# The second mixer of a two-layer AdaLN block: gates folded into diagonal matrix products

## The chip, the cores and the metric

The kernel runs on one core of a Trainium2 chip. The metric is the device time of one execution in microseconds. A core has five engines that work side by side and meet only through semaphores: TensorE (matrix products), VectorE, ScalarE, GpSimd (called POOL in the profile) and SyncE (SP), which here only starts DMAs. ScalarE and POOL start DMAs as well. Each engine, and each DMA queue, works through its own instructions in program order.

## The reference, cut to what matters

x is [4, 512, 512]: four batches of 512 tokens with 512 features. Two layers follow each other, and each modulates a LayerNorm with per-batch rows that come from a small product (`mod`):

```
for layer in (0, 1):
    sa, ca, ga, sb, cb, gb = rows of silu(c) @ wmod          # per batch, 512 each
    ga, gb = sign(.) * max(abs(.), 0.25)
    h = layernorm(x) * (1 + ca) + sa
    x = x + ga * mixer(h)
    h = layernorm(x) * (1 + cb) + sb
    x = x + gb * ffn(h)
```

Layer 0 has linear attention as its mixer and a mixture of experts as its feed-forward part. Layer 1 has a 2:4-sparsified gated feed-forward part, and this mixer, which is the subject here:

```
y = h @ M            # M = W_in.T * coefficients @ W_out.T, 512 x 512, made on the chip
mixer(h) = h + y * rsqrt(mean(y*y) + eps) * norm_w
```

So the second mixer's step is x + ga\*h + ga\*norm_w\*normalised(y).

## The kernel before, in words

The program has stages: A (attention, eight head groups in a loop, four batches in each), a front part with the router, 39 expert slots, `back()`, then stage C (the second mixer, `step_c(b)` for four batches b) and stage D (the last feed-forward part: four groups g of its inner columns, four batches in each, `step_d(g, b)`). `walk` calls the same sequence of functions for each engine, and each engine's version of `step_c` or `step_d` holds that engine's instructions in the order in which they run; this written order and the semaphores are all that schedules the work. A batch is four tiles (NT) of 128 tokens; the features are four chunks (NC) of 128.

Every float32 product is made from three fp32r products: both operands are split into a high and a low part, and `mm3` (L720 to L722) issues high\*high, high\*low and low\*high. The high part is written by ScalarE, the low part by VectorE or POOL.

Two PSUM banks, `TAIL`, form a ring whose places are numbered ahead by `plan_ring`. `ring_full` counts what TensorE has put into it, `ring_read` what has been read out, `ring_done` what is finished. A LayerNorm takes four places (four chunks transposed), in two halves. The chain of one LayerNorm (k, b), where k is 2 for the mixer of layer 1 and 3 for its feed-forward part, is:

1. VectorE: `bn_stats` (L1453) and `bn_aggr` over the batch, then the reciprocal root by three Newton steps on a 128x4 tile (L1431 to L1437, 11 small operations with the one that adds epsilon), each waiting for the one before it.
2. VectorE: `ln_apply` (L1476), (x - mean) \* rstd into `xn` (a view of `xnb`) or, for (2, 2) and (2, 3), into `xw`.
3. TensorE: the transposes (L751) into the ring.
4. ScalarE: `ln_out`, scale and bias (L1137, out of PSUM into `tmp`), then the high part of `hT` (L1141). POOL: the low part (L1982).

In `back()` TensorE makes M (L1006, in two halves), ScalarE and VectorE split it, and (2, 0) and (2, 1) are normalised. `step_c(b)` on TensorE makes y for four tiles (48 products, operands `M_` and `hT`) in six banks (`YB`) and then the transposes of the next LayerNorm, (2, 2), (2, 3), (3, 0), (3, 1) in turn. ScalarE squares y with a running sum. VectorE does steps 1 and 2 of the LayerNorm, a second root chain for y, and the scale pass (L1902) into `yn`, which POOL adds to x (L2253). The term ga\*h is made apart from that by `gated(b)` on VectorE: it multiplies the normalised tile by one row (L1508) and adds another (L1511), four operations each, and POOL adds the result to x (L2035). The rows (`crow`) are broadcast from DRAM to 128 partitions by DMAs of ScalarE's queue, three per batch. They are made by POOL in the first head group of stage A (`mod_rows`).

`step_d(0, 0)` and `step_d(0, 1)` still carry LayerNorms (3, 2) and (3, 3). A step of D has four product groups r (24 products for gate and up, L720 to L722 with `W1a` or `W1b`), silu on ScalarE (L1379), the product on VectorE (L1917), absolute values on ScalarE (L1371), the 2:4 selection on VectorE (L1935 to L1962), the high part `ad` on ScalarE (L1398), the low part on POOL, and one step later the tail: the down product, which uses `ad`, row scale and add to x. The weights of group 0 are split by ScalarE and POOL (`split_d`): quarters 0 and 1 during `step_c(2)`, 2 and 3 during `step_c(3)`.

On SP's queue the last head group of stage A issues row loads (L597) and reloads of x (L561); `back()` waits for the last expert sums and brings x back from DRAM (L683).

## Time and profile before

| | us |
|---|---|
| median of three timed runs | 2017.32 (2016.87 to 2019.9) |
| profiled execution, its own time | 2017.79 |
| its span | 2016.0 |
| TensorE busy | 1815.1 (90%) |
| VectorE busy | 1232.9 (61%) |
| ScalarE busy | 688.4 (34%) |
| POOL busy | 734.3 (36%) |

The times inside the span, here and in the rows below, count from the span's start. Busy shares are averages over stages with different limits, so the stage in question has to be read by itself: M is made from 1284 to 1312 us, stage C runs from 1337 to 1421 us, and stage D follows to the end. In a timeline row the columns are start, duration, engine, line, operation, output<-inputs and count; square brackets hold the idle time of the engine before it and what ended that. Several equal instructions in a row are merged into one with their count.

### The profile page before, as it was taken

What the parts mean: (1) busy time and instruction counts of PE and PEld (TensorE: products, weight loads), DVE (VectorE), ACT (ScalarE), POOL (GpSimd) and SP (SyncE); (2) the same over time, 40 slices, a digit from 0 to 9 for tenths busy, and PEclk for the clock granted to TensorE, in tenths of its full rate; (3) what the DMA queues carried; (4) which work ended last, traced back from release to release, by engine and by line L of the source; (5) the groups of instructions that cost most, each with busy time, mean ns of one, the idle gap of its engine ahead of it and who ended that gap; (6) DMA issues with size and microseconds to landing.
All of it is one profiled execution on the core that took longest, in us unless ns stands there. A gap on an engine that the chain in (4) does not pass through costs nothing.

```text
span 2016.0 us, 25506 instructions
## 1 busy us (share of the span) xinstructions
PE 1815.1 (90%) x8300; PEld 1423.6 (71%) x8300; DVE 1232.9 (61%) x2172; ACT 688.4 (34%) x1321; POOL 734.3 (36%) x717
## 2 busy tenths in 40 slices
PE   8989999999999999987549898957689999999996
PEld 5657888888888888866447676535477778787784
DVE  4557666666666666687754344389775757566564
ACT  2434454544454444432202232134333122213220
POOL 1436121212111122211343555357645445536442
PEclk9999999999999999998759999978799999999998
DMA  6211454535353535421387999600101011101011
GB/s 235 84 64 60 137 158 136 156 109 154 93 168 103 188 105 188 115 69 37 105 276 202 295 266 253 167 26 20 55 26 33 26 32 48 31 6 52 6 53 42
DMA packets 100194, 220.54 MB, mean 109 GB/s; under 512 B 6684, under 2 KB 31276, under 8 KB 98576
## 3 DMA queue, kind: packets, MB, share of 16 engines
q1 hardware_dynamic: 76160, 167.64, 26.3%
q0 software_dynamic: 11616, 28.98, 6.2%
q10 hardware_dynamic: 12336, 22.89, 3.7%
q8 instruction: 44, 0.72, 0.2%
q14 instruction: 38, 0.31, 0.0%
HBM read 128.11 MB, written 91.37 MB: 109 GB/s over the span
## 4 chain that ended last, share of the span: by engine, by line
PE 69%; DVE 18%; issue 6%; DMA 3%; ACT 2%; POOL 2%; ACTq 0%; POOLq 0%; DVEq 0%; SPq 0%
PE bank L720 21%; PE bank L722 20%; PE bank L721 20%; DVE hh L1962 2%; PE bank L911 2%; PE bank L786 2%; PE bank L1006 1%; DVE st L1453 1%; DVE rr L1723 1%; DMA u_d<-yt,sm 1%; PE bank L937 1%; DVE fl L1940 1%; DVE tmp L1715 1%; DVE na L1435 1%; DVE na L1434 1%
## 5 line engine op out<-in xcount | busy, mean ns | idle before, releaser
L1723 DVE RECIPROCAL rr<-rr 128x256 f32<-128x256 f32 x128 | 218.7, 1730 | 4.7 <-ACT num L1189 4.7
L720 PE MATMUL bank<-hT,W1b 128*128 128x512 f32 x512 | 210.5, 411 | 10.8 <-DVE hh L1917 10.8
L720 PE MATMUL bank<-W1a,hT 128*128 128x512 f32 x512 | 209.6, 409 | 3.4 <-DVE hT L1637 3.4
L721 PE MATMUL bank<-hT,W1b 128*128 128x512 f32 x512 | 205.1, 401 | 0.0
L722 PE MATMUL bank<-hT,W1b 128*128 128x512 f32 x512 | 204.8, 400 | 0.0
L722 PE MATMUL bank<-W1a,hT 128*128 128x512 f32 x512 | 201.4, 393 | 0.0
L721 PE MATMUL bank<-W1a,hT 128*128 128x512 f32 x512 | 200.7, 392 | 0.0
L2054 POOL TENSOR_TENSOR x<-x,tmp 128x512 f32<-128x512 f32 x64 | 101.3, 1583 | 261.3 <-DVE tmp L1715 261.3
L1917 DVE TENSOR_TENSOR hh<-hh,bank 128x512 f32<-128x512 f32 x64 | 43.2, 686 | 188.6 <-PE bank L722 159.2
L1742 DVE SCALAR_TENSOR_TENSOR kt<-bank,kt 128x256 fp32r<-128x256 f32 x128 | 50.8, 397 | 173.5 <-ACT vt L1205 173.4
L1982 POOL TENSOR_TENSOR W<-stage,W 128x1024 fp32r<-128x1024 f32 x32 | 76.8, 2400 | 189.6 <-ACT W L1097 187.3
L1204 ACT ACTIVATE kt<-bank 128x256 fp32r<-128x256 f32 x128 | 49.3, 385 | 235.1 <-PE bank L722 234.5
L1398 ACT ACTIVATE ad<-hh 128x512 fp32r<-128x512 f32 x64 | 40.3, 633 | 253.1 <-DVE hh L1962 253.1
L720 PE MATMUL bank<-W1b,ot 128*128 128x512 f32 x256 | 105.3, 412 | 22.8 <-DVE tmp L1712 14.2
L720 PEld LDWEIGHTS bank<-hT,W1b 128*128 128x128 f32 x512 | 98.3, 192 | 35.2 <-DVE hh L1917 13.7
L720 PEld LDWEIGHTS bank<-W1a,hT 128*128 128x128 f32 x512 | 96.9, 189 | 36.9 <-issue 16.3
L722 PEld LDWEIGHTS bank<-hT,W1b 128*128 128x128 f32 x512 | 98.0, 191 | 24.2
L721 PEld LDWEIGHTS bank<-hT,W1b 128*128 128x128 f32 x512 | 98.3, 192 | 20.0
L722 PEld LDWEIGHTS bank<-W1a,hT 128*128 128x128 f32 x512 | 96.8, 189 | 22.1
L720 PE MATMUL bank<-W,ad 128*128 128x512 f32 x256 | 102.8, 402 | 10.1 <-DVE ad L1969 8.9
L721 PEld LDWEIGHTS bank<-W1a,hT 128*128 128x128 f32 x512 | 97.4, 190 | 17.6
L1776 DVE SCALAR_TENSOR_TENSOR qt<-bank,qt 128x512 fp32r<-128x512 f32 x64 | 44.0, 690 | 101.5 <-ACT qt L1233 101.5
(265 smaller groups left out, 4596.8 us busy)
## 6 DMA issues: line engine op xcount, KB each, us to landing
hs_d<-bor SPq DMA_DIRECT2D x24, 1548.0 KB, 11.9
ws_d<-W SPq DMA_DIRECT2D x48, 512.0 KB, 6.2
WB<-ws_d SPq DMA_DIRECT2D x8, 3072.0 KB, 17.5
stage<-wa SPq DMA_DIRECT2D x32, 512.0 KB, 5.5
stage<-wbe SPq DMA_DIRECT2D x24, 512.0 KB, 4.3
stage<-wdn SPq DMA_DIRECT2D x24, 512.0 KB, 3.9
mw<-wmod SPq DMA_DIRECT2D x10, 1024.0 KB, 4.8
hg<-hs_d ACTq DMA_DIRECT2D x39, 258.0 KB, 4.5
```

The lines of the kernel that those rows point to most:

```text
L720: pe.matmul(o, lhs(HI), rhs(HI), start=start, stop=False, **kw)
L721: pe.matmul(o, lhs(HI), rhs(LO), start=False, stop=False, **kw)
L722: return pe.matmul(o, lhs(LO), rhs(HI), start=False, stop=stop, **kw)
L786: last = pe.matmul(o[0:NB, :], scT[:, layer, c, :], w[:, c * H:(c + 1) * H], start=c == 0, stop=c == NC - 1)
L911: last = pe.matmul(bank[NN[pair][head]][:, :], kvb[q, wl, pair, :], qt[q, wr, pair, :], start=i == 0, stop=i == 2)
L1204: act.activation(kt[:, t % 2, HI, :], bank[t % 2][:, 0:256], ACT.Relu)
L1723: dve.reciprocal(rr[:, pair, h], rr[:, pair, h]).then_inc(r_rec, 1)
L1742: dve.scalar_tensor_tensor(out=kt[:, t % 2, LO, :], in0=bank[t % 2][:, 0:256], scalar=0.0, in1=kt[:, t % 2, HI, :].bitcast(F32), op0=ALU.m ...
L1776: dve.scalar_tensor_tensor(out=qt[:, LO, pair, :], in0=bank[pair][:, :], scalar=0.0, in1=qt[:, HI, pair, :].bitcast(F32), op0=ALU.max, op1 ...
L1917: dve.tensor_tensor(hh[:, r, :], hh[:, r, :], bank[4 + r % 2][:, :], ALU.mult).then_inc(d_h, 1)
L1982: return pool.tensor_tensor(dst, src, hi.bitcast(F32), ALU.subtract)
L2054: pool.tensor_tensor(xt, xt, tmp[:, (key + t) % 2, :], ALU.add).then_inc(ring_done, 1)
```

## The change

- **The term ga\*h** is no longer made by VectorE and POOL. TensorE multiplies h (the same `hT` columns that feed y) by a diagonal matrix of ga per batch and chunk (`gated_h`): for each of four tiles, four chunks of 128 columns with three products each, into four ring places called "res". VectorE adds each place to x. The 16 diagonals (`dg`) are written by ScalarE (identity times a gate column) and VectorE (low part) in `back()`. The gate columns (`gcol`) come by four element-wise DMAs of SP's queue in the last head group. `gated`, `gated_add` and two of three broadcast rows go; the third is now loaded by SP (`crow_load`).
- **The LayerNorms (2, \*) and (3, \*)** are applied by ScalarE: Identity with scale rstd and bias -mean\*rstd, from x (`ln_scaled`).
- **Shared chains**: `c_scales` computes the reciprocal roots of one or two LayerNorms and of y in one chain on a wider tile, and the bias with one operation more. In `step_c` that chain stands behind the squares of y.
- **The normalised y** is added to x by VectorE and not by POOL.
- **Order**: the transposes of (3, 1), (3, 2), (3, 3) go into `step_d(0, 0)`, behind groups 0, 1 and 3, and `step_c(3)` has none. `step_d(0, 1)` carries no LayerNorm any more, so its absolute values follow each group. Weight quarters 0 and 1 are split at the start of `back()`, 2 and 3 behind the last "res" product of `step_c(3)`, because `dg` lies where `W1b` will be. `YB` has another order of banks, so that group 0 of D waits for 12 reads of y and group 1 for 16.

The diff, cut to its core. TensorE:

```diff
+            def gated_h(b):
+                n0 = RING[("res", b)]
+                pe.wait_ge(dg_lo, NC * (b + 1))
+                for t in range(NT):
+                    o = ring_slot(n0 + t, (n0 + t) % 2)
+                    for c in range(NC):
+                        last = mm3(o[:, c * P:(c + 1) * P], hcol(c, b, t), lambda h, c=c: dg[:, b, h, c, :],
+                                   c == 0, c == NC - 1, skip_group_check=True)
+                    last.then_inc(ring_full, 1)
...
                     last.then_inc(y_full, 1)
+                gated_h(b)
                 for half in range(2):
-                    ln_transposes(layernorms("C", 0, b), half)
+                    ln_transposes(C_LNS[b], half)
```

ScalarE:

```diff
             def back():
-                for i in range(SLOTS - NY, SLOTS):
-                    act.wait_ge(us_done[i % NY], added(i))
-                crows(0, 0)
-                crows(1, 0)
+                act.wait_ge(dn_full, SLOTS)
+                split_d(0, 0)
+                split_d(0, 1)
+                act.wait_ge(gcol_full, 16 * NB)
+                for b in range(NB):
+                    for c in range(NC):
+                        act.activation(dg[:, b, HI, c, :], ident[:, :], ACT.Copy, scale=gcol[:, c, b:b + 1]) \
+                            .then_inc(dg_hi, 1)
...
+            def ln_scaled(k, b):
+                p = (k - 2) * NB + b
+                act.wait_ge(c_scaled, p + 1)
+                if p >= 2:
+                    act.wait_ge(ring_full, ln_end(2 + (p - 2) // NB, (p - 2) % NB))
+                col = column((k, b))
+                for t in range(NT):
+                    last = act.activation(xn_of(k, b)[:, t, :], x[:, b * NT + t, :], ACT.Identity,
+                                          scale=crs[:, col + t:col + t + 1], bias=cnm[:, col + t:col + t + 1])
+                last.then_inc(xn_ready, 1)
...
+            def step_c(b):
+                if b > 0:
+                    ln_scaled(*((2, 3), (3, 0), (3, 1))[b - 1])
+                squares(b)
+                if b == 0:
+                    ln_scaled(2, 2)
+                if b == 3:
+                    act.wait_ge(ring_full, RING[("res", 3)] + NT)
+                    split_d(0, 2)
+                    split_d(0, 3)
+                if C_LNS[b]:
+                    ln_out(C_LNS[b], 0)
+                    ln_out(C_LNS[b], 1)
```

VectorE:

```diff
             def step_c(b):
-                ln = layernorms("C", 0, b)
-                stats(ln, range(NT))
-                ln_apply(*ln)
...
+                if b == 0:
+                    c_stats(2, 2)
+                    c_stats(2, 3)
+                    c_scales((2, 2), (2, 3), ("y", 0))
+                else:
+                    c_stats(3, b - 1)
+                    c_scales((3, b - 1), ("y", b))
+                n0 = RING[("res", b)]
+                for t in range(NT):
+                    n = n0 + t
...
+                    dve.wait_ge(ring_full, n + 1)
+                    xt = x[:, NT * b + t, :]
+                    dve.tensor_tensor(xt, TAIL[n % 2][:, :], xt, ALU.add).then_inc(ring_read, 1)
...
-                if gated_in("C", 0, b) is not None:
-                    gated(gated_in("C", 0, b))
+                for t in range(NT):
+                    n = NT * b + t
+                    dve.wait_ge(y_read, n + 1)
+                    xt = x[:, n, :]
+                    dve.tensor_tensor(xt, xt, yn[:, t, :], ALU.add).then_inc(c_add, 1)
```

POOL:

```diff
             def step_c(b):
-                for t in range(NT):
-                    n = NT * b + t
-                    pool.wait_ge(y_read, n + 1)
-                    xt = x[:, NT * b + t, :]
-                    pool.tensor_tensor(xt, xt, yn[n % 4], ALU.add).then_inc(c_add, 1)
-                ln_out(ln, 0)
-                ln_out(ln, 1)
...
-                gated_add(gated_in("C", 0, b))
+                n0 = RING[("res", b)]
+                for t in range(NT):
+                    pool.wait_ge(ring_done, n0 + t)
+                    pool.wait_ge(ring_read, n0 + t + 1)
+                    pool.tensor_tensor(mark[:, 2:3], mark[:, 0:1], mark[:, 1:2], ALU.add).then_inc(ring_done, 1)
```

## Rows read from the trace of the kernel before

**Rows 1.** Windows of two stretches: span, busy us (instructions) by engine, granted clock, DMA share, GB/s.

```profile
1312.00:1337.20 25.20, 5.98 (x32) 4.47 (x31) 18.05 (x33) 9.09 (x15) 13.09 (x10) 0.61 0.08 21
1337.20:1421.60 84.40, 58.73 (x258) 46.19 (x256) 80.69 (x169) 34.34 (x66) 56.14 (x39) 0.85 0.13 38
```

**Rows 2.** Waits of TensorE, 1284 to 1500 us: total, times, longest.

```profile
PE bank L751 <- DVE xnb L1476: 47.0, 4, 17.3
```

**Rows 3.** Groups on VectorE, 1284 to 1500 us: busy, mean ns, idle before.

```profile
L1511 DVE TENSOR_TENSOR xw<-xw,crow 128x512 f32<-128x512 f32 x8 | 14.8, 1904 | 0.0
L1508 DVE TENSOR_TENSOR xw<-xw,crow 128x512 f32<-128x512 f32 x8 | 12.7, 1648 | 0.0
...
L1508 DVE TENSOR_TENSOR xnb<-xnb,crow 128x512 f32<-128x512 f32 x8 | 11.1, 1448 | 6.5 <-PE bank L751 6.5
L1511 DVE TENSOR_TENSOR xnb<-xnb,crow 128x512 f32<-128x512 f32 x8 | 9.3, 1220 | 0.0
```

**Rows 4.** Timeline of TensorE's products.

```profile
1311.79 1.04 PE L751 MATMUL bank<-ident,xnb 128*128 128x128 f32 x8
...
1333.09 3.15 PE L751 MATMUL bank<-ident,xnb 128*128 128x128 f32 x12 [17.30 <-DVE xnb L1476]
...
1337.22 0.78 PE L720 MATMUL bank<-M_,hT 128*128 128x512 f32 x1
...
1374.68 0.40 PE L722 MATMUL bank<-M_,hT 128*128 128x512 f32 x1
1374.91 0.40 PE L720 MATMUL bank<-M_,hT 128*128 128x512 f32 x1
...
1421.65 0.47 PE L720 MATMUL bank<-hT,W1a 128*128 128x512 f32 x1 [0.84 <-issue]
...
1475.38 0.79 PE L720 MATMUL bank<-hT,W1b 128*128 128x512 f32 x1 [2.97 <-DVE hh L1917]
1475.97 0.63 PE L721 MATMUL bank<-hT,W1b 128*128 128x512 f32 x1
1476.39 0.63 PE L722 MATMUL bank<-hT,W1b 128*128 128x512 f32 x1
...
1494.01 0.47 PE L720 MATMUL bank<-W,ad 128*128 128x512 f32 x1 [1.01 <-ACT tmp L1137]
```

**Rows 5.** Timeline of 130-column products in stage A, and a weight load (PEld) among them.

```profile
600.12 0.28 PE L722 MATMUL bank<-vt,kt 128*128 128x130 f32 x1
600.24 0.27 PE L720 MATMUL bank<-vt,kt 128*128 128x130 f32 x1
...
600.17 0.19 PEld L720 LDWEIGHTS bank<-vt,kt 128*128 128x128 f32 x1
```

**Rows 6.** Groups on ScalarE, whole span, forms apart.

```profile
L1204 ACT ACTIVATE kt<-bank 128x256 fp32r<-128x256 f32 x128 | 49.3, 385 | 235.1 <-PE bank L722 234.5
...
L1137 ACT ACTIVATE tmp<-bank,modc 128x512 f32<-128x512 f32 x48 | 37.0, 771 | 83.6 <-issue 33.1 <-PE bank L751 25.2 <-POOL hT L1982 24.9
```

**Rows 7.** Costliest groups of the page: VectorE out of PSUM.

```profile
L1917 DVE TENSOR_TENSOR hh<-hh,bank 128x512 f32<-128x512 f32 x64 | 43.2, 686 | 188.6 <-PE bank L722 159.2
```

**Rows 8.** Timeline of VectorE.

```profile
1298.33 1.88 DVE L1453 BATCH_NORM_STATS2 st<-x 128x6 f32<-128x512 f32 x3 [13.05 <-DMA x<-u_d]
...
1405.54 1.21 DVE L1434 TENSOR_TENSOR na<-ve,rstd 128x4 f32<-128x4 f32 x1
1406.78 0.16 DVE L1435 SCALAR_TENSOR_TENSOR na<-na,rstd 128x4 f32<-128x4 f32 x1
...
1462.14 0.68 DVE L1935 TENSOR_TENSOR fl<-xnb 128x512 bf16<-128x512 f32 x1
```

**Rows 9.** Timeline of SP's DMA issues.

```profile
880.78 0.38 SPq L561 DMA_DIRECT2D x<-x_in  x1
```

**Rows 10.** Timeline of ScalarE, the last write of batch 1's LayerNorm.

```profile
1339.34 0.63 ACT L1141 ACTIVATE hT<-tmp 128x512 fp32r<-128x512 f32 x1
```

**Rows 11.** Timeline of POOL during the held operation of VectorE.

```profile
1404.19 2.54 POOL L1982 TENSOR_TENSOR hT<-tmp,hT 128x512 fp32r<-128x512 f32 x2
```

More of the change, by code:

```diff
@@ L125, in mod_uses, with column @@
     return ([(i - 1, "col")] if i > 0 and MOD_PARTS[i - 1] in COL_KIND else []) + [(i, "row")]
-def gated_in(stage, g, b):
-    return {1: 2, 3: 3}.get(b) if stage == "C" else None
+def column(what):
+    return NT * STATS.index(what)
 def tail_of(stage, g, b):
@@ L165, in plan_ring @@
                     halves = [("ln", *ln, 0), ("ln", *ln, 1)]
-                    parts = {"A": halves[:1] + parts + halves[1:], "C": parts + halves, "D": halves + parts}[stage]
+                    parts = halves[:1] + parts + halves[1:]
+                if stage == "C":
+                    parts = [("res", b)] + ([("ln", *C_LNS[b], h) for h in range(2)] if C_LNS[b] else [])
+                if (stage, g, b) == ("D", 0, 0):
+                    parts = [("ln", *ln, h) for ln in D_LNS.values() for h in range(2)]
                 if stage == "A" and g == 0:
@@ L1046, in step_d @@
                     need_h(3, b)
[L1047 to L1048 removed]
                 for r in range(4):
+                    if first and b == 0 and r < 2:
+                        pe.wait_ge(y_read, (NT * NB - 4, NT * NB)[r])
                     if b == 0:
@@ L1366, in absolute @@
                     if r == 0:
-                        if ln:
-                            act.wait_ge(ring_full, ln_end(*ln))
-                        if not (first and b == 0):
+                        if first and b == 0:
+                            act.wait_ge(ring_full, ln_end(3, 3))
+                        else:
                             act.wait_ge(d_sp, s * NSP)
@@ new lines, in matrix_lo @@
+            def matrix_lo(half):
+                for j in range(2):
+                    m = 2 * half + j
+                    dve.wait_ge(m_hi, m + 1)
+                    dve.tensor_tensor(M[:, LO, m, :], bank[((0, 1), (4, 5))[half][j]][:, :], M[:, HI, m, :].bitcast(F32),
+                                      ALU.subtract).then_inc(m_lo, 1)
+            def back():
+                diagonals()
+                c_stats(2, 0)
+                c_scales((2, 0))
+                matrix_lo(0)
+                c_stats(2, 1)
+                c_scales((2, 1))
+                matrix_lo(1)
@@ L2265, in step_d @@
                         split_d(g + 1, j)
-                ln = layernorms("D", g, b)
-                ln_out(ln, 0)
-                ln_out(ln, 1)
+                if isinstance(g, int) and g == 0 and b == 0:
+                    for ln in D_LNS.values():
+                        ln_out(ln, 0)
+                        ln_out(ln, 1)
                 tails("D", g, b)
```

251 lines of the change are left out of this document (116 added, 135 removed).

## The prediction

> **What bounds the kernel now.** The slices of the page show TensorE busy nearly everywhere except in two dips, and the later one is the second mixer and the start of the last stage, so I cut that stretch into windows. From 1337.2 to 1421.6 us VectorE is busy 80.7 of 84.4 us while TensorE is busy 58.7, and TensorE's granted clock is 0.61 in the stretch ahead and 0.85 in this one [rows 1]. The waits of TensorE say the same: 47.0 us of them were ended by VectorE's LayerNorm apply into one buffer alone, in four stops of up to 17.3 us [rows 2]. VectorE's groups in the same stretch show what stands in front of that apply: two passes over a gated tile per batch, 14.8 + 12.7 + 11.1 + 9.3 = 47.9 us in 32 operations [rows 3]. So here a microsecond off VectorE's queue is a microsecond off the end, until TensorE's own order takes over. After 1494 us TensorE runs without a stop worth the name, and whatever moves 1494.01 earlier moves the end by as much [rows 4].
>
> The sum is made against the profiled execution, 2017.8 us, of which 2016.0 are span. That is 0.5 us above the median of the three timed runs, 2017.3. 0.2%, what a measurement can tell from no change, is 4 us.
>
> **The change, part by part.**
>
> *Removed from VectorE:* the eight gated operations per batch, 48 us in all, the four-operation apply, and one of two reciprocal-root chains per batch (11 operations, 0.2 us apart when nothing holds them). *Removed from POOL:* the gated add and the add of the normalised output, 32 operations of the size of its subtractions, 1.27 us each at best.
>
> *Added to TensorE:* 48 small products per batch (4 tiles, 4 chunks, 3 precision parts, 128 columns). The nearest rows are products of 130 columns with the same weight load, which start 0.11 us apart (600.12 and 600.24) [rows 5]: 48 x 0.112 = 5.4 us a batch, 21.6 in all. The bounds are 0.06 us each (a quarter of the 0.23 us of 512 columns [rows 4]; 2.9 us a batch) and 0.19 us each, the weight load's own record (9.1 us a batch). I take 0.112, since width and operands are nearly equal. The Trainium skill, "TensorE: Matmul & The Clock Gate", section "The mechanism", says that a weight load overlaps products in flight only when its row group differs. Rival D works that case out from rows.
>
> *Added to ScalarE:* 32 applies of 128x512 with scale and bias. The nearest row is the same function at 0.77 us [rows 6], so 3.1 us a batch; bounds 0.6 and 0.8. Sixteen diagonals of 128x128: below the 0.385 us of 128x256 [rows 6], about 0.27, 4.3 us. VectorE's 16 low parts: well below the 0.69 us of 128x512 [rows 7], about 0.3, 5 us. These and the two weight splits moved in front of them (2 us on ScalarE, 4.9 on POOL) lie between the last expert product at 1284 and the landing of x, which starts VectorE at 1298.33 after 13.05 idle us [rows 8]. I take their cost as nothing; if the cover went, they would still be under TensorE's matrix product, which runs to 1311.8.
>
> *Added to VectorE:* per batch four adds out of PSUM and four scale passes (0.69 each [rows 7]) and four adds with both inputs in SBUF, 0.68 each alone (the first step of the selection, 1462.14) [rows 8].
>
> *DMA and queues:* four loads of the gate columns, 2048 single elements, on SP's queue in the last head group. They stand ahead of the reload of x that is issued at 880.78 [rows 9] and waits for the tail of an earlier batch, by some 25 us (a head group's step): nothing, and each of the four would have to take 6 us to reach it. Twelve row broadcasts leave ScalarE's queue, four come on SP's; each has 18 us before its use. POOL's row arithmetic in the first head group shrinks by three operations off the path.
>
> **Leg 1, matrix product to first output product.** Before: 1311.79 to 1337.22. The transposes of batch 0 stay where they are. ScalarE needs 6.9 us from their start to its last write (1333.09 to 1339.34 + 0.63 in the next batch [rows 4, 10]), so it is free at 1318.7, applies batch 1's LayerNorm in 3.1, and the transposes then take 4.1 (1333.09 to 1337.22). First product at 1326.0: 11.2 us earlier. The matrix product itself and the wait for x are untouched.
>
> **Leg 2, the four steps.** TensorE's queue is in order: output products (48 x 0.23 = 11.0 us), gated tiles, transposes. Gated tiles 0 and 1 need 2.7 us, but tile 2 needs tile 0's bank back, and VectorE reads it only behind its shared chain: square 1.0 after the last product, chain 12 x 0.2 = 2.4, add 0.7, handover 0.1, so tile 2 starts at +4.2 instead of +2.7. Tiles 2 and 3 end at +6.9, VectorE's last read at +7.7, ScalarE's alternation with the transposes frees TensorE at +10.5. A step is 21.5, and I add 1 for stretches at the lower of the two clock levels (1.2 and 2.4 GHz), which show as products 0.43 us apart (1475.97 to 1476.39, after a stop of 2.97 us) instead of 0.23 [rows 4]: 22.5. Three steps and a last one without transposes (11 + 7): 85.5, so the last stage begins at 1411.5. Before, this leg took 84.4 (1337.22 to 1421.65 [rows 4]). The products that the change adds use up what the idle time gives back: this leg is worth -1 us. VectorE's own turn is 7.7 + 2.7 + 5.7 (adds beside POOL) + 2.9 (statistics) = 19 us, inside 22.5 with 3 to spare.
>
> **Leg 3, to the first tail.** Before: 72.4 us (1421.65 to 1494.01), with a stop for batch 2's LayerNorm in it. Now four product groups (5.5 each, 24 x 0.23) and three transposes (4.1), twice 1.0 waiting for ScalarE's apply: 36.3, to 1447.8. Late next is the 2:4 selection: ScalarE ends the LayerNorm writes at 1450.6, has two absolute values at 1451.9, and from there to the released product of the next batch it took 13.2 us before (1462.14 to 1475.38 [rows 4, 8]): 1465.1. TensorE has done the next two groups at 1458.8 and stands 6.3 us, where it stood 2.97. The next two groups then take 14.1 instead of 11, as they did at 0.43 us apart. First tail at 1479.2, before 1494.0.
>
> Sum: 11.2 - 1.1 + 4.7 = 14.8 us. **Forecast 2017.8 - 14.8 = 2003.0.**
>
> **The rivals.**
>
> *A, VectorE still bounds the steps (chance 0.20).* The turn of 19 us holds only if the SBUF adds cost 1.4 us. The gated passes beside POOL averaged 1.2 to 1.9 [rows 3]. At 1.9, and with some of the statistics' small operations held, the turn is 24 to 25, the step about 25: 3 x 2.5 later, 2010.5. Against it: POOL has lost half of its work.
>
> *B, the chain is held on TensorE's path (0.06); this one ends slower.* A two-input operation took 1.21 us where the next one took 0.16 [rows 8], while POOL's subtractions of 1.27 us were running [rows 11]. The chain now stands between the output products and gated tile 2 in every step. The Trainium skill, "SBUF — State Buffer", Terms, says the port pair of VectorE and GpSimd is locked for a whole instruction and the loser blocks; by that rule the trace agrees. If 8 of 12 operations are held in each step, 8 x 1.05 x 4 = 34 us: 2037. It decides from 14.8 / 4 = 3.7 us a step, four held operations. Against: POOL's subtractions for a batch end about 8 us before the next chain starts.
>
> *C, the last stage gives it back (0.07).* If the selection is held by POOL as well, the stop of 6.3 us becomes 12: 2009.
>
> *D, weight loads don't overlap (0.02).* Each small product would cost 0.19 + 0.11 = 0.30 us, 14.4 a batch instead of 5.4, 36 us over four: 2024. The rows exclude it as far as 130-column products go: a load of 0.19 us lies inside products that start 0.11 apart [rows 5]. By the skill's sentence it would be so; the trace does not agree.
>
> *E, smoother than I count (0.15).* No step at the lower clock and the stop in leg 3 under 3 us: 3 + 3 + 3 less, 1994 to 1998. The change not doing what it says can be excluded: the passes are gone from VectorE's queue.
>
> **How the numbers follow.** Forecast case 0.50 (1998 to 2008), A 0.20, E 0.15, C 0.07, B 0.06, D 0.02. Range 1996 to 2012: it takes the forecast case, C, most of A and E. Faster by over 0.2% (below 2013.3): 0.50 + 0.15 + 0.07 + 0.16 of A = 0.88. Same: 0.05, from A's upper end and a mild B. Slower: 0.07.
>
> **What would show it.** Right: the first output product near 1326, steps of 21.5 to 23.5 us, small products 0.11 us apart, the last stage from about 1411, the first tail near 1479, TensorE's waits for the LayerNorm apply almost gone. Wrong: small products over 0.15 us apart; chain operations of over 1 us between the squares and the first PSUM add; steps of 25 with VectorE full; a diagonal ending after 1311; the first tail later than 1488.

## The result, and the profile after

The changed kernel takes 2002.79 us (median of four runs, 2002.44 to 2004.78), the kernel before 2017.09 us on the same chip. The ratio is 0.9924, with a 95% interval of 0.9909 to 0.9939, so the kernel is faster by 0.76%. The span of the profiled run fell from 2016.0 to 2000.9 us, by 15.1. All medians and ratios, here and below, are of executions in the faster of the two states that a core shows; one execution of the kernel with one product part (2108.9 us) and one of the kernel before (2327.1) were in the slower one and are left out.

To compare kernels I cut their traces at the same four products of TensorE. The **segment** runs from the first product of the matrix M to the first tail product of the last stage. It has three legs, as in the prediction: up to the first output product, the four steps of stage C, and the last stage up to its first tail. Below is the timeline of TensorE after the change, with the marks of these legs and the rows between them that the argument needs.

```profile
1283.36 0.59 PE L1030 MATMUL bank<-mst 128*128 128x512 f32 x1
...
1320.56 3.15 PE L775 MATMUL bank<-ident,xnb 128*128 128x128 f32 x12 [5.74 <-ACT xnb L1373]
...
1324.33 0.48 PE L744 MATMUL bank<-M_,hT 128*128 128x512 f32 x1
...
1335.41 0.22 PE L744 MATMUL bank<-dg,hT 128*128 128x128 f32 x1
...
1335.58 0.28 PE L746 MATMUL bank<-dg,hT 128*128 128x128 f32 x1
1335.69 0.27 PE L744 MATMUL bank<-dg,hT 128*128 128x128 f32 x1
...
1339.58 0.33 PE L744 MATMUL bank<-dg,hT 128*128 128x128 f32 x1 [1.38 <-DVE x L1970]
...
1340.75 0.41 PE L745 MATMUL bank<-dg,hT 128*128 128x128 f32 x1
1340.96 0.42 PE L746 MATMUL bank<-dg,hT 128*128 128x128 f32 x1
...
1347.70 0.48 PE L744 MATMUL bank<-M_,hT 128*128 128x512 f32 x1
...
1411.97 0.73 PE L744 MATMUL bank<-hT,W1a 128*128 128x512 f32 x1
...
1466.76 0.79 PE L744 MATMUL bank<-hT,W1b 128*128 128x512 f32 x1 [7.49 <-DVE hh L1989]
...
1479.72 0.39 PE L744 MATMUL bank<-W,ad 128*128 128x512 f32 x1
```

The kernel before started M at 1284.33. With [rows 4] the legs are:

| | before | after | forecast |
|---|---|---|---|
| leg 1, M to first output product | 52.9 | 41.0 (-11.9) | -11.2 |
| leg 2, the four steps | 84.4 | 87.6 (+3.2) | +1.1 |
| its steps | 21.5, 15.4, 25.9, 21.6 | 23.4, 22.8, 22.2, 19.3 | 22.5 three times, 18 |
| leg 3, to the first tail | 72.4 | 67.8 (-4.6) | -4.7 |
| segment | 209.7 | 196.4 (-13.3) | -14.8 |

The rest of the 15.1 us is 1.0 ahead of M and 0.8 behind the first tail. The three legs of the changed kernel as windows (columns as in [rows 1]):

```profile
1283.36:1324.33 40.97, 33.31 (x98) 16.44 (x96) 28.05 (x78) 22.41 (x42) 13.40 (x12) 0.92 0.48 147
1324.33:1411.97 87.64, 81.89 (x436) 70.28 (x434) 52.95 (x114) 41.53 (x77) 25.95 (x31) 0.89 0.03 10
1411.97:1479.72 67.75, 55.07 (x241) 43.39 (x242) 31.87 (x53) 36.47 (x55) 31.11 (x21) 0.92 0.13 39
```

Against the second window of [rows 1], which is leg 2 of the kernel before, the idle engine is now VectorE: it is busy 53 of 87.6 us instead of 81 of 84.4, and TensorE 82 instead of 59. The waits of TensorE from 1270 to 1500 us (total, times, longest) answer to [rows 2]:

```profile
PE bank L744 <- DVE hh L1989: 7.5, 1, 7.5
PE bank L775 <- ACT xnb L1373: 6.4, 2, 5.7
PE bank L775 <- ACT tmp L1171: 6.0, 12, 1.0
PE bank L744 <- DVE x L1970: 5.1, 4, 1.4
```

The 47.0 us of waits for the LayerNorm apply into xnb have become 6.4. In their place stand four short stops, one a step, behind y's chain and the first residual add (`x L1970`), and one stop of 7.5 us in the last stage. VectorE and ScalarE in step 0, and VectorE's adds of the normalised output in step 1, from their timelines:

```profile
1336.40 0.17 DVE L1928 TENSOR_SCALAR cst<-csum 128x4 f32<-128x4 f32 x1 [17.35 <-ACT sqj L1383]
...
1338.73 0.17 DVE L1936 SCALAR_TENSOR_TENSOR cst<-cmv,cst 128x8 f32<-128x8 f32 x1
1338.84 1.29 DVE L1970 TENSOR_TENSOR x<-bank,x 128x512 f32<-128x512 f32 x2
...
1369.85 6.16 DVE L1982 TENSOR_TENSOR x<-x,yn 128x512 f32<-128x512 f32 x4
```

```profile
1317.59 2.91 ACT L1373 ACTIVATE xnb<-x,cst 128x512 f32<-128x512 f32 x4
```

The chain takes 2.4 us and no operation of it is held; an apply on ScalarE takes 0.73 us. VectorE's adds of the normalised output are another matter. While POOL makes the low parts of the next LayerNorm, four of them take 6.16 us, 1.54 each. In the run below in which VectorE applies LayerNorm, the same four in step 0 take 2.49 us.

### The profile page after: what moved, and what is told of

Its sections match the earlier page's. It is cut to its first block and busy times, and to the rows that moved or that the text cites. A ratio compares the mean times of both kernels' runs of the same rounds, so it can differ in the third digit from the quotient of the medians.

```text
span 2000.9 us, 25863 instructions
## 1 busy us (share of the span) xinstructions
PE 1842.2 (92%) x8492; PEld 1450.2 (72%) x8492; DVE 1191.6 (60%) x2112; ACT 716.7 (36%) x1369; POOL 686.3 (34%) x697
## 5 line engine op out<-in xcount | busy, mean ns | idle before, releaser
L744 PE MATMUL bank<-hT,W1b 128*128 128x512 f32 x512 | 208.9, 408 | 14.8 <-DVE hh L1989 14.8
L744 PE MATMUL bank<-W1a,hT 128*128 128x512 f32 x512 | 209.7, 410 | 3.4 <-DVE hT L1657 3.4
L1989 DVE TENSOR_TENSOR hh<-hh,bank 128x512 f32<-128x512 f32 x64 | 43.4, 686 | 195.4 <-PE bank L746 166.0
L744 PE MATMUL bank<-W1b,ot 128*128 128x512 f32 x256 | 104.8, 410 | 23.0 <-DVE tmp L1732 14.8
```

The lines of the kernel that those rows point to most:

```text
L744: pe.matmul(o, lhs(HI), rhs(HI), start=start, stop=False, **kw)
L1989: dve.tensor_tensor(hh[:, r, :], hh[:, r, :], bank[4 + r % 2][:, :], ALU.mult).then_inc(d_h, 1)
```

## The experiments

Each run is compared with the kernel before on its own chip. On these chips it took 2018.7 us (the two edits of the kernel before, the adds on POOL, LayerNorm on VectorE), 2019.0 (both moves taken back), 2021.4 (chains separate, residual adds first, the two earlier LayerNorms) or 2021.0 (the other three), so the medians can't be compared with each other, only the ratios. The segment is that of one profiled execution. Leg 1 repeats well (41.0 in the runs that leave it alone, 41.3 in three of them). Leg 3 is 66.4 to 68.0 us in the changed kernel and the four runs that edit neither it nor the adds and applies ahead of it, so a difference of about 1 us in a segment says little. The whole times need several executions each, since what lies outside the segment scatters by more.

| run | median us | ratio, 95% interval | leg 1 | leg 2 | leg 3 | segment |
|---|---|---|---|---|---|---|
| before | 2017.1 | 1 | 52.9 | 84.4 | 72.4 | 209.7 |
| before, gated term left out | 1987.9 | 0.985 (0.983 to 0.987) | 42.8 | 71.6 | 60.1 | 174.5 |
| before, adds on VectorE | 2012.3 | 0.996 (0.995 to 0.998) | 52.8 | 81.1 | 67.5 | 201.4 |
| **changed** | 2002.8 | 0.992 (0.991 to 0.994) | 41.0 | 87.6 | 67.8 | 196.4 |
| adds on POOL | 2007.4 | 0.994 (0.991 to 0.997) | 41.0 | 92.3 | 69.5 | 202.7 |
| LayerNorm on VectorE | 2002.7 | 0.992 (0.990 to 0.993) | 37.4 | 93.0 | 64.0 | 194.3 |
| both moves taken back | 2005.7 | 0.993 (0.992 to 0.994) | 37.4 | 94.0 | 65.2 | 196.6 |
| chains separate | 2002.5 | 0.990 (0.989 to 0.992) | 41.0 | 86.4 | 68.0 | 195.4 |
| one product part of three | 1995.3 | 0.987 (0.985 to 0.989) | 41.3 | 81.6 | 67.1 | 190.0 |
| POOL kept busy | 2016.2 | 0.998 (0.997 to 0.999) | 41.3 | 101.1 | 68.0 | 210.4 |
| residual adds first | 1993.0 | 0.985 (0.984 to 0.987) | 41.3 | 76.2 | 69.1 | 186.7 |
| LayerNorm (2,1) earlier | 2001.8 | 0.991 (0.989 to 0.993) | 37.6 | 89.5 | 66.4 | 193.6 |
| LayerNorm (3,3) earlier | 1999.0 | 0.990 (0.988 to 0.993) | 41.0 | 87.8 | 64.1 | 192.9 |
| four changes of order | 1982.0 | 0.981 (0.980 to 0.983) | 37.6 | 77.3 | 60.0 | 174.9 |

**What the gated term costs, in the kernel before.** The two passes, the gated add and their row loads are taken out:

```
 def gated(b):
     ...
-    for t in range(NT):
-        dve.tensor_tensor(xg[:, t, :], xg[:, t, :], crow[:, 0, :], ALU.mult).then_inc(pq_mul, 1)
-    for t in range(NT):
-        dve.tensor_tensor(xg[:, t, :], xg[:, t, :], crow[:, 1, :], ALU.add).then_inc(pq_sum, 1)
 def gated_add(b):
     ...
-        pool.tensor_tensor(xt, xt, xn_of(2, b)[:, t, :], ALU.add).then_inc(pq_add, 1)
```

> The kernel before, with the term ga*h left out: the gated passes of VectorE, their adds on POOL and their row loads are gone, everything else stays (so x misses that term). Theory (the gated passes bound the old stage): the first output product comes about 12 us earlier, a step of stage C falls from 21 to about 16 us, the stop for the LayerNorm in the last stage shrinks; in all about 40 us less, 1977 us (1970 to 1985). Rival (the serial LayerNorm and root chains bound it, and the change won by moving and sharing them): less than 10 us gained, over 2007.

The segment is 35.2 us shorter, the kernel 30. That is less than the 40 expected, and 1988 us lies outside the range given, but far from the rival's 2007: the passes were on the path, as [rows 2, 3] had been read. 35.2 us for passes of 47.9 us says that part of them had cover; how much can't be had by subtraction, since the adds on POOL went too, and since durations hold waits (see the next run). With everything else left in its order, the 35.2 us bound what another way to compute ga\*h could win.

**One move alone, on the kernel before.** The normalised output is added by VectorE, behind its scale pass:

```
 def step_c(b):                       # VectorE
     ...
+    ...                              # for b < 3 behind POOL's gated add of the same batch
+    for t in range(NT):
+        dve.tensor_tensor(xt, xt, yn[n % 4], ALU.add).then_inc(c_add, 1)
 def step_c(b):                       # POOL
-        pool.tensor_tensor(xt, xt, yn[n % 4], ALU.add).then_inc(c_add, 1)
```

> The kernel before, with one part of the change alone: the normalised y is added to x by VectorE and not by POOL. Theory (VectorE bounds the old stage, so each operation put on it is paid): four adds more per batch at 0.7 to 1.4 us, 4 x 2.7 to 4 x 5.6 = 11 to 22 us, less what POOL's smaller load gives back: 2027 us (2022 to 2034). Rival (POOL's add is what delays the statistics of the next LayerNorm, so this part helps by itself): 2012 or less.

The theory of a slower kernel was wrong: it is faster, by 0.36%, and by 8.2 us in the segment. Sixteen more operations were put on the engine that bounds it, and it finished sooner. The groups on VectorE from 1284 to 1500 us (busy us, mean ns | idle before) show how:

```profile
L1911 DVE TENSOR_TENSOR x<-x,cs 128x512 f32<-128x512 f32 x8 | 14.0, 1785 | 0.0
...
L1911 DVE TENSOR_TENSOR x<-x,ct 128x512 f32<-128x512 f32 x8 | 10.7, 1381 | 0.0
...
L1508 DVE TENSOR_TENSOR xw<-xw,crow 128x512 f32<-128x512 f32 x8 | 7.2, 954 | 0.0
L1511 DVE TENSOR_TENSOR xw<-xw,crow 128x512 f32<-128x512 f32 x8 | 7.1, 946 | 0.0
L1434 DVE TENSOR_TENSOR na<-ve,rstd 128x4 f32<-128x4 f32 x36 | 5.8, 162 | 1.2
```

The adds cost 24.7 us. But the passes over xw fell from 27.5 us [rows 3] to 14.3, and the small operation of the chain from this row of the kernel before, same view, to half of it:

```profile
L1434 DVE TENSOR_TENSOR na<-ve,rstd 128x4 f32<-128x4 f32 x36 | 11.2, 310 | 1.2
```

With the other small operations the chains fell from 37.6 us to 22.6 (L1431 to L1437), and with the passes that is 28.2 us less, more than the adds cost. The rival, that POOL's add delays the next statistics, is not what the trace shows: VectorE has no wait for POOL in that stretch in either run, the time is in the durations. POOL had done its adds of 1.29 to 1.52 us during the passes and the chains; that these adds held both is the reading that fits, and the run with POOL kept busy tests it. The durations in a trace hold these waits, so the busy time of an engine isn't a quantity of work that can be added and subtracted.

**The same move, taken back from the changed kernel.**

```
-    for t in range(NT):              # VectorE
-        dve.wait_ge(y_read, n + 1)
-        dve.tensor_tensor(xt, xt, yn[:, t, :], ALU.add).then_inc(c_add, 1)
+    for t in range(NT):              # POOL, step_c, ahead of the LayerNorm's low parts
+        pool.wait_ge(y_read, n + 1)
+        pool.tensor_tensor(xt, xt, yn[:, t, :], ALU.add).then_inc(c_add, 1)
```

> The changed kernel, with that part alone undone: the normalised y is added to x by POOL, in front of its LayerNorm low parts, as it was before. Theory: POOL's adds end 15 to 16 us after the last output product instead of its low parts at 14, the low part of the first transposed chunk comes about 7 us later, and ScalarE may not fill the second place of its buffer before that; TensorE's transposes and with them three steps grow by about 6 us: 2020 us (2012 to 2026). Rival (VectorE's adds cost on its own turn, so giving them back helps): 2000 or less.

The direction held in the segment and the size did not: 6.4 us, not 17. The whole times alone can't tell this run from the changed kernel (0.991 to 0.997 against 0.991 to 0.994). POOL and ScalarE in step 0 and behind it, from their timelines, show the way it takes:

```profile
1343.29 5.01 POOL L2308 TENSOR_TENSOR x<-x,yn 128x512 f32<-128x512 f32 x4 [0.41 <-DVE yn L1975]
1348.26 2.54 POOL L2048 TENSOR_TENSOR hT<-tmp,hT 128x512 fp32r<-128x512 f32 x2
```

```profile
1349.67 0.78 ACT L1171 ACTIVATE tmp<-bank,modc 128x512 f32<-128x512 f32 x1 [4.12 <-POOL hT L2048]
...
1352.35 2.92 ACT L1373 ACTIVATE xnb<-x,cst 128x512 f32<-128x512 f32 x4
1355.17 0.57 ACT L1383 ACTIVATE sqj<-bank 128x512 bf16<-128x512 f32 x1
```

POOL's adds delay its low parts, these hold ScalarE's third eviction for 4.12 us, behind it stands the apply and behind the apply stand the four squares. So y's chain starts 1.6 us behind the first small product of step 1 instead of 1.0, the stop of TensorE for it is 1.88 us instead of 1.24, and tiles 2 and 3 take 4.4 us instead of 3.8.

**LayerNorm applied by VectorE**, the other move taken back:

```
-        last = act.activation(xn_of(k, b)[:, t, :], x[:, b * NT + t, :], ACT.Identity, scale=..., bias=...)
+        last = dve.tensor_scalar(xn_of(k, b)[:, t, :], x[:, b * NT + t, :], crs[...], cnm[...], ALU.mult, ALU.add)
```

> The changed kernel, with the LayerNorm apply of stages C and D back on VectorE (0.54 us an operation instead of 0.77 on ScalarE), shared chains and diagonal products kept. Theory (moving the apply was not what won, and in leg 1 it even costs, since ScalarE comes to batch 1's apply only behind batch 0's writes): first output product 4 us earlier, the first step 2 us longer since the apply stands behind the adds out of PSUM, 1 to 2 us less in the last stage: 2000 us (1996 to 2004). Rival (the apply on ScalarE is a main part of the gain): over 2008.

The whole time is as expected, its parts less so. The applies stand in VectorE's queue right behind their chains, but (2,2) behind the adds out of PSUM. Leg 1 is without the 3.6 us in which ScalarE applied (2,1) behind its evictions, and step 0 gives them back with interest: 28.4 us against 23.4, 5 us longer and not 2. Leg 3 is 3.7 us shorter and not 1 to 2. For the whole the move to ScalarE is worth nothing here: 194.3 against 196.4 us, and a ratio with nearly the same interval.

**Both moves taken back**, so that the diagonal products, the shared chains and the change's new order are left:

> The changed kernel with both of its moves taken back, LayerNorm applied by VectorE and the normalised output added by POOL, so that of the change the diagonal products (and the shared chains) alone are left. Theory (the parts add up, each read from the run in which it alone was taken back: 202.7 us with the add on POOL, 194.3 us with LayerNorm on VectorE, against 196.4 us): 202.7 - 2.0 = 200.7 us for the segment, 9 us less than the kernel before, and 2007 us (2004 to 2010). Rival (VectorE's applies and POOL's adds hold each other, as the kernel before showed with its adds on POOL; the two moves are worth more together than apart): a segment of 204 us or more, 2010 to 2016 us, with applies of LayerNorm of over 1 us each where POOL adds.

For the segment neither held: it is 196.6 us, the 196.4 of the changed kernel, where adding up had given 200.7. (The median of 2005.7 us lies in the theory's range, but the changed kernel would take some 2003.6 on this chip, and the two ratios overlap.) So **the two moves bring nothing together, and the rest of the change brings 13.1 of the 13.3 us**. The hold that the rival named did happen while POOL made its adds: four applies took 1.31 us each, where four others beside an idle POOL took 0.48. But with LayerNorm on VectorE and the adds left there, the same four took 1.48 beside POOL's low parts, so the adds on POOL brought no more of it. From VectorE's timeline of this run in step 0:

```profile
1354.58 5.25 DVE L1926 TENSOR_SCALAR xnb<-x,cst 128x512 f32<-128x512 f32 x4
```

What the two moves share may be ScalarE's slack. With the adds on POOL, ScalarE's evictions are still held for 3.6 us in this run, but no apply of 2.9 us stands behind them, and the chain of step 1 starts 1.0 us behind the first small product, as in the changed kernel. No run takes that slack alone, so this is a reading and not a test. The adds on VectorE are worth 6.4 us where ScalarE applies LayerNorm, and 2.3 (196.6 - 194.3) where it does not: the second move mostly pays for the first.

The 13.1 us look like a simple difference: the gated term costs 35.2 us in its old form, and in its new one 192 small products at 0.116 us, 22.3, which leaves 12.9. The legs show that this agreement is partly luck. Against the kernel before without the gated term, this run is 27.6 us longer in legs 2 and 3, not 22.3, and 5.4 us *shorter* in leg 1 (37.4 against 42.8), though neither has a pass there. Those 5.4 us come from a part of the change that its description does not name. In `back()` VectorE used to make the low parts of both halves of M before it turned to LayerNorm (2,1). Now (2,1) stands between the two halves, in time in which VectorE would wait for the second, and the transposes of (2,1) find their input ready. In the kernel before without the gated term TensorE still waits for it:

```profile
1325.25 1.11 PE L751 MATMUL bank<-ident,xnb 128*128 128x128 f32 x4 [7.23 <-DVE xnb L1464]
```

So of the 13.1 us an estimated 5.4 belong to this order and some 8 to the diagonal products with the rest (13.1 - 5.4 = 7.7). No run has the diagonal products in the old order, so the split is not tested.

**Chains separate:**

```
-                    c_scales((3, b - 1), ("y", b))
+                    c_scales((3, b - 1))
+                c_scales(("y", b))
```

> The changed kernel with separate root chains: the LayerNorm's before the wait for the squares of y, y's alone behind it. Theory (sharing saves VectorE operations that lie in its idle time, 3 to 4 us a step, so it is worth nothing here): from the start of the matrix product to the first tail product 196.4 us as in the changed kernel, within 1 us. Rival (sharing is a part of the gain, 2.2 us a step): 203 us or more.

The segment is 1.0 us shorter, at the edge of the 1 us that the theory allowed and as near to nothing as this can be read. The eleven operations that the shared chain saves lay in VectorE's idle time, which is 3 to 4 us a step.

**The price of the small products.** The gated product with one part of three (the two mixed ones left out):

```
-                        last = mm3(o[:, c * P:(c + 1) * P], hcol(c, b, t), lambda h, c=c: dg[:, b, h, c, :], ...)
+                        last = pe.matmul(o[:, c * P:(c + 1) * P], hcol(c, b, t)(HI), dg[:, b, HI, c, :], ...)
```

> The changed kernel with the gated output product ga * h computed from the high parts alone: 16 small products a batch instead of 48, so the two mixed terms of the split product are left out and the result is less exact. Theory (the small products cost 0.11 to 0.12 us each wherever TensorE has work, and lie on its path): 32 x 0.116 = 3.7 us less work a step; a part of it goes into the stop for y's chain, which VectorE sets, so 2 to 3.7 us a step and 8 to 13 us in all: 1990 to 1995 us. Rival (a step ends with VectorE's turn, and the small products only fill its wait): less than 3 us in all, 2000 to 2003.

The two measures differ. The segment is 6.3 us shorter, between theory and rival; the ratio is 0.987 against 0.992, about 11 us, inside the theory's 8 to 13, and the median of 1995.3 us is just past the range given. The profiled execution is the slowest of the three (2002.2, the others 1993.9 and 1995.3), and what the others won outside it is not known. In it, the waits of TensorE in the steps (1335 to 1420 us) say where most of the other 8.5 of the 14.8 us that 128 small products take went:

```profile
PE bank L1044 <- DVE x L1970: 12.3, 4, 3.2
```

The stop behind y's chain grew from 5.1 to 12.3 us. With fewer products TensorE mostly arrives earlier at a point that VectorE sets. That point, more than the number of small products, bounds the steps: the first three fell by 0.6 to 1.3 us each, and only the last, which has no transposes behind it, by 3.0.

**POOL kept busy beside the chain**, the price of rival B:

```
+                pool.wait_ge(y_sq, NT * (b + 1))
+                for _ in range(6):
+                    chained(pool.tensor_tensor(junk[:, :], junk[:, :], junk[:, :], ALU.add))
```

> The changed kernel with six additions of 128x256 bf16 on POOL, on a scratch tile that nothing reads, issued in each of the four steps as soon as the squares of the step are summed, beside y's chain on VectorE. Nothing waits for them. Theory (a VectorE instruction whose operands all lie in SBUF is held while one of POOL's runs): single operations of the chain take 0.4 to 1 us instead of 0.16, the chain 2 to 5 us longer, and TensorE's stop for x or for the gated tiles longer by as much: 1 to 4 us a step, 2007 to 2019 us. Rival (the operation of 2.37 us seen beside POOL's split in the run with the adds first has another cause): all operations of the chain stay at 0.16 us, 2002 to 2004 us.

The theory held: 2016.2 us, and 14.0 us more in the segment, 210.4 where the kernel before had 209.7. VectorE's and POOL's timelines in step 0:

```profile
1339.09 0.61 DVE L1929 TENSOR_SCALAR cst<-csum 128x4 f32<-128x4 f32 x1 [17.85 <-ACT sqj L1384]
1339.74 0.17 DVE L1931 TENSOR_SCALAR cst<-cst 128x12 int32<-128x12 int32 x1
1339.94 0.47 DVE L1933 TENSOR_TENSOR cst<-cst 128x12 f32<-128x12 f32 x1
1340.44 0.17 DVE L1934 SCALAR_TENSOR_TENSOR cst<-cst 128x12 f32<-128x12 f32 x1
1340.65 0.47 DVE L1935 SCALAR_TENSOR_TENSOR cst<-cst 128x12 f32<-128x12 f32 x1
1341.15 0.17 DVE L1933 TENSOR_TENSOR cst<-cst 128x12 f32<-128x12 f32 x1
```

```profile
1339.07 4.16 POOL L2309 TENSOR_TENSOR junk<-junk 128x256 bf16<-128x256 bf16 x6 [8.06 <-ACT sqj L1384]
```

Every second operation of the chain is held, and the one at its head too. Two of them with their gaps take 0.71 us (1339.94 to 1340.65), and POOL's additions come 0.69 us apart (six in 4.16): the chain runs at POOL's pace. 24 additions that nothing waits for, 16.6 us of POOL's time at that pace, and the gain in the segment is gone; of the whole time 0.2% of 0.8% is left. The Trainium skill, "SBUF — State Buffer", section "SBUF: two separate sides", says that a VectorE operation with two SBUF inputs and one of GpSimd lock the shared port pair for a whole instruction, and that whichever starts first blocks the other. The trace agrees for those operations. The held one at the head (`cst<-csum`, 0.61 us) has one input and is not of that kind; whether an addition of POOL was held in turn can't be read from it.

**The stop in each step taken out.** y's chain stands behind the four residual adds, which are what frees the banks for the gated tiles. For that it is separate from the LayerNorm's chain, as in the run with chains separate:

```
-                    c_scales((3, b - 1), ("y", b))
+                    c_scales((3, b - 1))
                 ...
                 for t in range(NT):
                     ...
                     dve.tensor_tensor(xt, TAIL[n % 2][:, :], xt, ALU.add).then_inc(ring_read, 1)
+                c_scales(("y", b))
```

> The changed kernel with separate chains, and VectorE's four adds out of the ring moved in front of y's chain. Theory (gated tile 2 waits for the add of tile 0 only because the chain stands before it, and the stop of 1.3 us also brings a stretch at the lower clock): the four stops of 1.25 to 1.38 us go, gated tiles 2 and 3 take 2.8 us each pair instead of 3.1 to 4.4, the stretch from the matrix product to the first tail product is 5 to 10 us shorter than 196.4. Rival (the two-bank ring or the transposes bound the step anyway): 195 or more.

Confirmed: 9.7 us less than the changed kernel and 8.7 less than the run with chains separate, with steps of 20.1, 19.9, 19.9 and 16.4, and the 48 small products of a batch in 5.5 us without a stop. In the run with chains separate the stops were these:

```profile
PE bank L744 <- DVE x L1971: 4.2, 4, 1.1
```

Leg 2 with the residual adds first, as a window:

```profile
1326.88:1403.09 76.21, 72.77 (x435) 62.72 (x433) 51.62 (x132) 40.99 (x76) 23.50 (x30) 1.00 0.03 11
```

For the same products TensorE is busy 72.8 us instead of 81.9, as its granted clock is 1.00 instead of 0.89 (with chains separate it is 0.89 too). In its last step POOL's weight splits met the chain. VectorE's and POOL's timelines:

```profile
1404.30 0.16 DVE L1932 TENSOR_TENSOR cst<-cst 128x4 f32<-128x4 f32 x1
1404.49 2.37 DVE L1933 SCALAR_TENSOR_TENSOR cst<-cst 128x4 f32<-128x4 f32 x1
1406.90 0.16 DVE L1934 SCALAR_TENSOR_TENSOR cst<-cst 128x4 f32<-128x4 f32 x1
1407.10 2.30 DVE L1932 TENSOR_TENSOR cst<-cst 128x4 f32<-128x4 f32 x1
```

```profile
1404.43 4.95 POOL L2054 TENSOR_TENSOR W1b<-stage,W1b 128x1024 fp32r<-128x1024 f32 x2
```

Two operations of the chain are held for 4.4 us, and TensorE stands 1.1 us for the normalised output ahead of the last stage's second group. So in the last step of the run with four changes two adds stand ahead of the chain and two behind it.

**ScalarE applies (2,1) right behind (2,0)**, where it waits for M's second half anyway:

```
                     if half == 0:
                         ln_scaled(2, 0)
+                        ln_scaled(2, 1)
                 ln_out((2, 0), 0)
                 ln_out((2, 0), 1)
-                ln_scaled(2, 1)
```

> The changed kernel with one line moved: ScalarE applies LayerNorm (2, 1) right behind (2, 0), while TensorE still makes the second half of M, and not behind the writes of (2, 0). Theory (the 2.9 us of that apply are on the path of leg 1): first output product 3.6 us earlier counted from the start of the matrix product, 37.4 us instead of 41.0, and the stretch to the first tail product 192.8. Rival (batch 0's low parts on POOL would hold the first output product anyway): 40 us or more.

Leg 1 is 37.6 us, as expected; of the 3.3 won, leg 2 takes 1.9 back. The segment of 193.6 us holds 1.4 in leg 3, which the edit doesn't touch.

**LayerNorm (3,3) one group earlier** in the last stage:

```
-D_LNS = {0: (3, 1), 1: (3, 2), 3: (3, 3)}
+D_LNS = {0: (3, 1), 1: (3, 2), 2: (3, 3)}
```

with its statistics behind the first product group instead of the second.

> The changed kernel with the last LayerNorm (3, 3) one product group earlier: its statistics behind VectorE's first product, its transposes behind group 2 instead of group 3. Theory (the absolute values, and with them the 2:4 selection, wait for its writes, and that makes the stop of 7.5 us before group 2 of the next batch): the stop falls to 3 or 4 us, the stretch to the first tail product is 3 to 5 us shorter than 196.4. Rival (the selection is late because of the last product group and not of the LayerNorm): the stop stays over 6 us.

Confirmed. The segment is 3.5 us shorter; the whole time (0.988 to 0.993) can't tell it from the changed kernel. The waits of TensorE from 1440 to 1500 us show the stop of 7.5 us as one of 4.1:

```profile
PE bank L744 <- DVE hh L1989: 4.1, 1, 4.1
```

**Four changes of order together:** the last three and this one, behind the squares of step 3:

```
                 squares(b)
+                if b == 3:
+                    ln_scaled(3, 2)
```

> The changed kernel with four changes of order together: the four residual adds stand ahead of y's chain in VectorE's queue (in the last step two ahead of it and two behind), ScalarE applies LayerNorm (2,1) right behind (2,0), it applies (3,2) right behind the squares of step 3, and (3,3) is emitted one group earlier in the last stage. Theory (each takes out a stop of its own, and the stops lie one behind another on TensorE): first output product 37.5 us behind the start of M's product instead of 41.0; steps of about 20, 20, 20 and 16 us instead of 23.4, 22.8, 22.3 and 19.3; 62 to 64 us from the last stage to the first tail instead of 67.8. The segment of 196.4 us falls to 176 to 180, the kernel to 1985 (1981 to 1989). Rival (the stops share a cause, so that one gain eats the other, for instance since ScalarE's applies now meet the gated evictions): no better than the adds ahead of the chain alone, a segment of 186.7 and 1993 us.

The theory held, a little on the good side: 1982.0 us, a segment of 174.9 (176 to 180 expected), which is 21.5 us less than the changed kernel and 34.8 less than before. Its legs 2 and 3 as windows:

```profile
1320.21:1397.46 77.25, 73.79 (x434) 63.44 (x433) 56.57 (x148) 43.83 (x80) 23.30 (x29) 0.98 0.04 11
1397.46:1457.48 60.02, 52.87 (x242) 42.07 (x242) 28.79 (x56) 33.72 (x51) 32.19 (x22) 0.97 0.15 45
```

In leg 2 TensorE is busy 73.8 us instead of 81.9 for the same products: its granted clock is 0.98 instead of 0.89. The single gains are 9.7, 2.8 and 3.5 us, 16.0 together. The other 5.5 are left for the apply of (3,2) and the split adds of the last step, which were not run alone, and for what the edits do to each other. What is left of waits from 1270 to 1480 us is mostly ScalarE's eviction of the transposes:

```profile
PE bank L775 <- ACT tmp L1171: 10.2, 18, 1.0
PE bank L744 <- DVE hh L1997: 3.0, 1, 3.0
```

## Why the prediction was right, and where its reasons were not

**The number** came out within 0.3 us of the median, 2003.0 against 2002.79. That is closer than its terms were, and the last microseconds of the agreement are luck. The legs erred by -0.7, +2.1 and +0.1 us, the changes outside the segment, -1.8 us, had been left out, and the two nearly cancel.

**What bounds the kernel.** That VectorE's passes stood on TensorE's path held. The sentence "a microsecond off VectorE's queue is a microsecond off the end" did not: 47.9 us of passes came to 35.2. The run with the adds moved to VectorE put 24.7 us on that queue and came out 6 us faster: how long VectorE's operations take depends on what POOL does beside them. The forecast was not hurt, as it was built from TensorE's order and not from VectorE's busy time.

**Leg 1** held: -11.9 against -11.2. ScalarE applied LayerNorm in 2.9 us (3.1 taken) behind its evictions, as described. The prediction put this down to the change as a whole; the runs show that LayerNorm on ScalarE makes this leg 3.6 us longer than it would be otherwise, and that about 5.4 us of what it wins come from VectorE's new order in `back()`, of which the prediction does not speak.

**Leg 2** is the term that was mis-sized: +3.2 instead of +1.1. The steps were built right: the chain starts 1.0 us behind the output products, takes 2.4, and tile 2 starts at +4.2 us (1335.41 to 1339.58), as forecast. The failed step is "I add 1 for stretches at the lower of the two clock levels". Behind each stop of only 1.2 to 1.4 us, the 24 products of tiles 2 and 3 took 4.35, 3.75, 3.14 and 4.33 us where tiles 0 and 1 take 2.79: 4.4 us over the four steps for tiles alone, where the forecast had allowed 3 for three steps and nothing for the last, which came out 1.3 us longer than forecast. The timeline shows it as products 0.21 us apart (1340.75, 1340.96) instead of 0.11 (1335.58, 1335.69).

**The small products** cost 0.116 us each (24 in 2.79 us, the end of the last one included; their starts are 0.11 apart), 0.112 taken. The row of 130 columns [rows 5] was the right neighbour. Rival D falls with that, at 0.30 us each. Its sum was also wrong: 36 us on top of 2003 are 2039, not 2024. By the sentence that the prediction quotes (the Trainium skill, "TensorE: Matmul & The Clock Gate", section "The mechanism"), taken by itself, it would have come about; the trace does not agree with it. The same section also lets a load into the background weight buffer be pulled ahead of products in flight, and by that it need not.

**The diagonals** took VectorE 0.58 us each, 9.3 in all beside POOL's weight splits, instead of 5. They ended as x landed (1295.19 us, and x at 1295.2), so that the statistics started without the idle time of before, and cost nothing, as said; but the cover was used to its end, which the estimate had not shown.

**Leg 3** held: -4.6 against -4.7, with a stop of 7.5 us where 6.3 was forecast, and 13.0 for the two groups behind it (1466.76 to 1479.72) where 14.1 was: two errors of about a microsecond that cancel. That the 2:4 selection would be late next was right.

**The rivals.** A (VectorE bounds the steps) did not come about by its turn: VectorE had 3.3 us idle ahead of the square of step 1. But the run with a third of the small products shows that a step is still bound by VectorE, through the point at which its chain stands and not by its load, which is what neither the forecast case nor A had said. B did not come about since POOL runs nothing beside the chain in stage C; the run with POOL kept busy shows that the mechanism is real, at 14 us, and the condition, "POOL's subtractions end about 8 us before the next chain starts", was the right one (7.0 us, 1352.82 to 1359.78). C did not come about beyond 1.2 us, E not at all.

**The parts of the change.** The diagonal products, which take the passes off VectorE, bring the gain together with the new order in `back()`. LayerNorm on ScalarE and the adds on VectorE bring nothing that can be measured together, though the second loses 6.4 us when it is taken back alone. The shared chains bring nothing when taken back alone. The prediction priced each as if it stood for itself. The other changes of order (the transposes moved into the last stage, the weight splits, the banks of y) were not run by themselves.

## What to carry to other kernels

When a move frees an engine, ask at which point of its queue the next engine waits, before asking how busy it is: here four changes of order, with no work removed, won 1.1% on top of the 0.8% of the change. Price an edit by taking it back alone and together with its neighbours; here one move looked worth 6.4 us and the other a loss of 2.1, and together they were worth 0.2. And compare windows cut at the same products, not at the same times: the stages shift under a fixed window. Last, keep POOL's SBUF additions away from chains of small operations on VectorE, even those that nothing waits for.

## What was not expected of the hardware

- An operation of VectorE on 128x4 elements takes 0.16 us alone and 2.37 beside POOL's split of 2.5 us; one on 128x12 takes 0.17 and 0.47 beside POOL's additions, which come 0.69 us apart. Six such additions a step, 16.6 us of POOL's time in all, cost 14.0 us of the segment.
- Moving 16 additions from POOL to VectorE, the fuller engine, made the kernel before 0.36% faster.
- Stops of TensorE as short as 1.24 us were followed by stretches at the lower of the two clock levels (1.2 GHz), up to 24 small products long. With the stops gone the granted clock of stage C rose from 0.89 to 1.00. That pays more than the stops themselves: with chains separate they were 4.2 us, and removing them won 8.7.
